# Expert combine over three engines one group apart, early beta, stores by group, unrolled limit search

## The chip, the cores and the metric

The kernel runs on one core of a Trainium2 chip. The time is that of the device for one execution, in microseconds; less is better. The engines are PE (TensorE), DVE (VectorE), ACT (ScalarE), POOL (GpSimd) and SP (SyncE, which here only issues DMAs).

## The reference

A chain of eight residual layers works on `x`, 16 sequences of 256 tokens with 128 features, in float32. Each layer is `x = x + f(layernorm(x))`: gated linear attention with a gated FFN, a linear layer with quantised operands, causal attention, a mixture of experts, rotary attention, a ternary MLP, a selective scan, and a second mixture of experts. The two mixtures matter here.

```python
# first mixture (L1_ffn): 4096 tokens, 8 experts, top 2, capacity by order of arrival
y[t] = sum_k gate[t, k] * out[expert[t, k], slot[t, k]]          # x = x + y

# second mixture (L3_ffn): capacity 768 for each expert, filled by descending gate value
pv, pp = lax.top_k(prio, capacity)                               # prio: gate value, -1 elsewhere
h     = gelu(xin @ w1 + b1);  out_e = (h @ w2 + b2) * w
out   = zeros.at[tok].add(out_e)
out   = (out - mean(out)) / sqrt(var(out) + 1e-5) * ln_g + ln_b  # x = x + out
```

## The kernel before

The program is a list of layers. Each is a `Block` in which every engine has its own written-out stream, with semaphores between the streams; a block ends in a barrier of all engines (line L57 in the profile). `sig.close()` then runs another block in which GpSimd clears the layer's semaphores one after the other. `x` stays in SBUF as 32 tiles of 128 tokens by 128 features.

`router` (for the first and, with `by_weight`, the last mixture) normalises the tiles on ScalarE, computes the logits and ranks them on VectorE. For the last mixture it then searches each expert's limit, the 768th largest gate, bit by bit: `STEPS` = 15 steps of two bits. In a step VectorE makes three candidates (`cand`), counts per candidate the values that reach it (`seen`, `counts`), PE adds the counts over partitions, and VectorE keeps the bits whose count is large enough (`keep`, `gain`, `prefix`). Both engines run the steps in a hardware loop (`Fori`), with waits whose value grows by a register. Every step depends on the one before.

`experts` runs 16 units (two halves of eight experts) of transposes, `hidden` and `result` on PE, with activations on ScalarE, `turned` (`xT`) and `result` (`y`, which adds b2) on VectorE, and scatters to `results` in DRAM by GpSimd. Its order on PE and VectorE is `turned(u+1)`, then `result(u-1)`.

After the last scatter comes the combine, in `NGROUP` = 8 groups of `GT` = 4 tiles. SP loads for each group the two expert rows of every token (`got`, three buffers) and waits from the fourth group on until `used` frees a buffer. VectorE does all else: the first product by the gate (in the first mixture with `x` added), the second product and sum, `bn_stats` and `bn_aggr` for the layernorm that follows (first mixture) or for the layernorm of the result (last mixture). In the last mixture it goes on: variance plus epsilon (`ve`), a wait for GpSimd's power -0.5 (`rs`), normalisation, times `ln_g`, plus `ln_b`, plus `x`. There is one `acc`, and a group is finished before the next begins. When all is done, a block of its own (`store`) writes `x` to the output in one DMA of 2 MB.

Of the kernel before, what the change touches and what calls it, by code (L numbers as in the profile page):

```python
# [13 lines left out]
ALU = mybir.AluOpType  # L14
# [4 lines left out]
P = 128  # L19
# [3 lines left out]
LN_EPS = 1e-5  # L23
# [1427 lines left out]
def router(nc, g, name, w, bias, by_weight, cap, queue):  # L1451
# [48 lines left out]
    with nc.Block() as block:  # L1500
        @block.vector
        def _(dve):
# [52 lines left out]
            if by_weight:  # L1555
# [11 lines left out]
                with dve.Fori(0, STEPS) as b:  # L1567
# [121 lines left out]
        def _(pe):  # L1689
# [19 lines left out]
            if by_weight:  # L1709
# [21 lines left out]
def experts(nc, g, name, w1, b1, w2, b2, last, cap, queue, results):  # L1731
# [13 lines left out]
    acc = sb("acc", [P, GT, P])  # L1745
    st, mv = sb("st", [P, GT, 6]), sb("mv", [P, GT, 2])
    rs, ve = sb("rs", [P, GT]), sb("ve", [P, GT])
# [4 lines left out]
    back, used = sig("back", 3), sig("used")  # L1752
    sum_ready, x_ready, st_ready, mv_ready, ve_ready, rs_ready, ln_ready = (
        sig("sum"), sig("x"), sig("st"), sig("mv"), sig("ve"), sig("rs"), sig("ln"))
    H, Y, T = g.pb[0:4], g.pb[4:6], g.pb[6:8]

    with nc.Block() as block:
        @block.sync
        def _(sp):
# [9 lines left out]
            for i in range(NGROUP):  # L1769
                if i >= 3:  # L1770
                    sp.wait_ge(used, i - 2)
                for k in range(2):
# [3 lines left out]
                        .then_inc(back[i % 3], 16)  # L1776

        @block.gpsimd
        def _(pool):
# [8 lines left out]
            if not last:  # L1788
                return
            with pool.Fori(0, NGROUP) as i:  # L1790
# [12 lines left out]

# [40 lines left out]
        def _(dve):  # L1844
# [12 lines left out]

            turned(0)
# [5 lines left out]
            flat = acc[:, :, :].rearrange("p t d -> p (t d)")  # L1864
            for i in range(NGROUP):
                cols = slice(i * GT * P, (i + 1) * GT * P)
                dve.wait_ge(back[i % 3], 32 * (i // 3 + 1))
                for t in range(GT):
                    gate = g.gate[:, 0, i * GT + t:i * GT + t + 1]
                    if last:  # L1870
                        ins = dve.tensor_scalar(acc[:, t, :], got[i % 3][0][:, t, :], gate, None, ALU.mult)
                    else:
                        ins = dve.scalar_tensor_tensor(out=acc[:, t, :], in0=got[i % 3][0][:, t, :], scalar=gate,
                                                       in1=g.x[:, i * GT * P + t * P:i * GT * P + (t + 1) * P],
                                                       op0=ALU.mult, op1=ALU.add)
                ins.then_inc(sum_ready, 1)
                dve.wait_ge(sum_ready, 2 * i + 1)
                for t in range(GT):
                    gate = g.gate[:, 1, i * GT + t:i * GT + t + 1]
                    out = acc[:, t, :] if last else g.x[:, i * GT * P + t * P:i * GT * P + (t + 1) * P]  # L1880
                    ins = dve.scalar_tensor_tensor(out=out, in0=got[i % 3][1][:, t, :], scalar=gate,
                                                   in1=acc[:, t, :], op0=ALU.mult, op1=ALU.add)
                ins.then_inc(sum_ready, 1)
                dve.wait_ge(sum_ready, 2 * i + 2)
                dve.memset(g.scrap[:, 0:1], 0.0).then_inc(used, 1)
                for t in range(GT):
                    out = acc[:, t, :] if last else g.x[:, i * GT * P + t * P:i * GT * P + (t + 1) * P]
                    ins = dve.bn_stats(st[:, t, :], out)
                ins.then_inc(st_ready, 1)
                dve.wait_ge(st_ready, i + 1)  # L1890
                for t in range(GT):
                    out = mv[:, t, :] if last else g.mv[:, 2 * (i * GT + t):2 * (i * GT + t) + 2]
                    ins = dve.bn_aggr(out, st[:, t, :])
                ins.then_inc(mv_ready, 1)
                dve.wait_ge(mv_ready, i + 1)
                if last:
                    dve.tensor_scalar(ve[:, :], mv[:, :, 1], LN_EPS, None, ALU.add).then_inc(ve_ready, 1)
                    dve.wait_ge(rs_ready, i + 1)
                    for t in range(GT):
                        ins = dve.tensor_scalar(acc[:, t, :], acc[:, t, :], mv[:, t, 0:1], rs[:, t:t + 1],  # L1900
                                                ALU.subtract, ALU.mult)
                    ins.then_inc(ln_ready, 1)
                    dve.wait_ge(ln_ready, i * 4 + 1)
                    dve.tensor_tensor(acc[:, :, :], acc[:, :, :],  # L1904
                                      g.l3_ln_g[:, :].unsqueeze(1).broadcast_to([P, GT, P]), ALU.mult)\
                        .then_inc(ln_ready, 1)
# [1328 lines left out]
class Globals:  # L3235
    pass


def store(nc, g, out):

    sig = Signals(nc, "store")
    stored = sig("stored")
# [179 lines left out]
```

## Time and profile before

| | |
|---|---|
| runs of the kernel | 2951.98 us median of 3 (2951.33 to 2956.23) |
| profiled execution | 2951.07 us, span 2949.2 us |
| busy: PE, DVE, ACT, POOL | 75%, 62%, 43%, 40% of the span |
| limit search | 2611.60 to 2658.96 us of the span |
| first combine, VectorE | 1402.37 to 1431.72 us |
| last combine, VectorE | 2872.89 to 2937.10 us |
| from there to the end of the span | 12.1 us |

The busy shares are means over twelve layers with different limits. The positions are microseconds from the start of the span, which is the profiled execution without what lies before and behind it on the device. A timeline merges neighbouring instructions of one line into one row with their number; the bracket gives the engine's idle time ahead of it and what ended it. "SPq" is a DMA issued by SP.

### The profile page before, as it was taken

The page shows a single profiled execution, that of the slowest core. Times are in us where ns is not written, and L with a number is a line of the kernel's source. Part 1 is how long each engine was busy: PE and PEld are TensorE (multiplying, and loading weights), DVE is VectorE, ACT ScalarE, POOL GpSimd, SP SyncE. Part 2 cuts the span into 40 slices and gives each one's busy share as a digit, 9 for nine tenths or more (in the row PEclk, how much of TensorE's full clock was granted, in tenths as well). Part 3 has the DMA queues.
Part 4 walks back from the last instruction along what each step waited for, and adds up shares of the span by engine and source line. Part 5 has one row for each costly group of instructions (what it writes and reads, how often), then busy time and mean ns, then how long its engine had stood idle before and what let it go on. Part 6 is the DMA issues. An engine that isn't in the chain of part 4 may idle for free. (4 is left out here: it accounts for less than half of the span.)

```text
span 2949.2 us, 46603 instructions
## 1 busy us (share of the span) xinstructions
PE 2197.5 (75%) x15036; PEld 1518.3 (51%) x15036; DVE 1830.9 (62%) x4981; ACT 1253.6 (43%) x2698; POOL 1185.2 (40%) x1211
## 2 busy tenths in 40 slices
PE   2799999999988885078289896959999999730480
PEld 0566666666667674056155554846666666430360
DVE  3678787878767854011656664748988888752016
ACT  1454545454523264022045553736666666320230
POOL 2433333333311002735112121557777777515441
PEclk9899999999999586589588887979999999855695
DMA  7300000000010000122323222000000000001122
GB/s 215 115 1 0 0 0 0 0 0 0 0 62 4 0 1 3 52 60 62 96 65 80 70 74 77 0 1 1 0 0 0 0 0 0 0 1 35 53 77 65
DMA packets 105859, 93.80 MB, mean 32 GB/s; under 512 B 12268, under 2 KB 92294, under 8 KB 105606
## 3 DMA queue, kind: packets, MB, share of 16 engines
q1 hardware_dynamic: 98086, 76.85, 9.4%
q0 software_dynamic: 7680, 15.81, 1.6%
q8 instruction: 47, 0.77, 0.1%
q14 instruction: 46, 0.38, 0.0%
HBM read 62.15 MB, written 46.26 MB: 37 GB/s over the span
## 5 line engine op out<-in xcount | busy, mean ns | idle before, releaser
L2993 POOL TENSOR_SCALAR mb_w<-mb_duT,mb_bT 128x256 f32<-128x256 f32 x512 | 466.8, 932 | 121.6 <-PE bank L3003 65.0
L2928 DVE TENSOR_TENSOR_SCAN mb_hs<-mb_dA,bank 128x512 f32<-128x512 f32 x256 | 300.9, 1205 | 37.8 <-issue 24.8
L38 POOL TENSOR_TENSOR scrap<-ones 128x1 f32<-128x1 f32 x64 | 12.4, 194 | 749.0 <-DVE gla_ss L420 487.0
L3022 PE MATMUL bank<-mb_hc,ident 128*128 128x512 f32 x512 | 262.2, 636 | 13.2 <-DVE mb_hc L2938 12.5
L2150 DVE TENSOR_REDUCE ra_mx<-bank 128x2 f32<-128x512 f32 x256 | 166.9, 688 | 101.9 <-PE bank L2027 100.1
L2984 ACT ACTIVATE mb_dA<-mb_delta,mb_A 128x255 f32<-128x255 f32 x512 | 216.6, 495 | 9.2 <-DVE mb_hs L2928 9.0
L2236 ACT ACTIVATE ra_pT<-bank 128x512 f32<-128x512 f32 x256 | 139.4, 595 | 131.8 <-PE bank L2047 130.7
L1801 ACT ACTIVATE e_hid<-bank,e_b 128x512 f32<-128x512 f32 (+1 forms) x128 | 81.2, 634 | 234.9 <-PE bank L1820 231.9
L3003 PE MATMUL bank<-ident,mb_w 128*128 128x128 f32 x1024 | 151.4, 282 | 34.3 <-DVE mb_hs L2928 26.2
L1812 PE MATMUL bank<-ident,e_x 128*128 128x128 f32 x112 | 18.8, 292 | 205.4 <-DMA e_x<-queue 205.4
L1784 POOL DMA_INDIRECT results<-e_y,e_x x112 | 107.2, 957 | 144.3 <-DVE e_y L1855 119.3
L2938 DVE TENSOR_TENSOR mb_hc<-mb_hs,bank 128x1024 f32<-128x1024 f32 x128 | 153.0, 1195 | 0.0
L3003 PEld LDWEIGHTS bank<-ident,mb_w 128*128 128x128 f32 x1024 | 120.7, 146 | 50.0 <-issue 34.3
L546 DVE COPY_PREDICATED gla_sT<-c_seen,bank 128x384 f32<-128x384 int32 x256 | 134.7, 579 | 12.1 <-issue 12.1
L3022 PEld LDWEIGHTS bank<-mb_hc,ident 128*128 128x128 f32 x512 | 92.9, 202 | 94.9 <-issue 67.9
L1849 DVE COPY e_xT<-bank 128x512 f32<-128x512 f32 (+1 forms) x32 | 19.7, 616 | 188.2 <-PE bank L1812 188.1
L532 DVE TENSOR_TENSOR gla_qm<-bank,gla_ex 128x256 f32<-128x256 f32 x128 | 54.0, 422 | 123.3 <-ACT gla_en L514 123.3
L1855 DVE TENSOR_TENSOR e_y<-bank,e_b 128x512 f32<-128x512 f32 (+1 forms) x32 | 20.0, 625 | 166.4 <-PE bank L1830 166.4
L2027 PE MATMUL bank<-ra_k,ra_q 48*128 48x256 bf16 x512 | 97.7, 304 | 33.8 <-DMA ra_q<-rope_rows 28.1
L1812 PEld LDWEIGHTS bank<-ident,e_x 128*128 128x128 f32 x112 | 14.4, 152 | 207.7 <-DMA e_x<-queue 206.8
L2046 PE MATMUL bank<-ra_q,ra_k 48*128 48x256 bf16 x512 | 111.4, 298 | 10.7 <-ACT ra_neg L2229 9.4
L387 ACT ACTIVATE gla_az<-gla_az 128x512 f32<-128x512 f32 x64 | 40.3, 630 | 178.6 <-DVE gla_az L415 178.6
(521 smaller groups left out, 6112.7 us busy)
## 6 DMA issues: line engine op xcount, KB each, us to landing
results<-const_empty SPq DMA_DIRECT2D x2, 4096.0 KB
e_got<-results SPq DMA_DIRECT2D x32, 256.0 KB, 3.2
rope_rows<-ra_part SPq DMA_DIRECT2D x48, 128.0 KB, 1.9
ra_k<-rope_rows SPq DMA_DIRECT2D x32, 192.0 KB, 3.3
ra_q<-rope_rows SPq DMA_DIRECT2D x32, 192.0 KB, 4.2
queue<-const_spare_rows SPq DMA_DIRECT2D x1, 4128.0 KB
e_x<-queue SPq DMA_DIRECT2D x8, 516.0 KB, 4.0
e_w<-in_L_ffn_w SPq DMA_DIRECT2D x2, 2048.0 KB, 7.8
```

Of the source, the lines that this page charges most:

```text
L546: dve.copy_predicated(sT[b][:, hd, :], g.seen[:, :], SC[hd][:, 0:3 * P]).then_inc(sc_ready, 1)
L1784: pool.indirect_dma_start(out=results[:, :], in_=y[u % YR][:, t, :], in_offset=None, out_offset=bass.IndirectOffsetOnAxis(ap=x[e % XR][:, ...
L2027: ins = pe.matmul(MX[a][:, t * 256:(t + 1) * 256], qz[k][rows, p, t * P:(t + 1) * P], kk[k][rows, p, :], start=True, stop=True)
L2046: pe.matmul(out, kk[k][rows, p, t * P:(t + 1) * P], qz[k][rows, p, :], start=True, stop=False)
L2150: dve.tensor_reduce(mx[:, :, a, p], halves(MX[a]), AXX, ALU.max).then_inc(mx_ready, 1)
L2236: act.activation(pT[p % 4][a][:, :, :], halves(SB[a]), ACT.Exp, scale=SC).then_inc(p_ready, 1)
L2928: dve.tensor_tensor_scan(hs[n // 2 % 2][:, n % 2, :, :].rearrange("p c t -> p (c t)"), dA[n % RD][:, :, :].rearrange("p c t -> p (c t)"), ...
L2938: dve.tensor_tensor(hc[grp % 2][:, :, :, :], hs[grp % 2][:, :, :, :], RC[grp % 2][:, :].rearrange("p (n t) -> p n t", n=2).unsqueeze(2) .b ...
L2984: ins = act.activation(dA[n % RD][:, c, 1:SEQ], delta[k][:, c, 1:SEQ], ACT.Exp, scale=A[:, c, n:n + 1])
L2993: ins = pool.tensor_scalar(w[n % RH][:, h, :], duT[k][:, h, :], bT[k][:, h, n:n + 1], None, ALU.mult)
L3003: ins = pe.transpose(DB[n % 2][:, c * 256 + h * P:c * 256 + (h + 1) * P], w[n % RH][:, h, c * P:(c + 1) * P], g.ident[:, :])
L3022: ins = pe.matmul(YB[:, :], g.ident[:, :], hc[grp % 2][:, j, :, :].rearrange("p c t -> p (c t)"), start=(n == 0), stop=(n == NS - 1))
```

## The change

The limit search is written out in Python loops on VectorE and PE; its instructions are the same.

In the combine, the first product goes to ScalarE (`first`, into `part`). In the first mixture GpSimd adds `x` to it (`joined`). VectorE adds the second product (`summed`) and takes the moments one group later. In the last mixture ScalarE normalises (`normalised`, as `rs * acc + nmr`, with `nmr` = -mean times rs made by VectorE in `shifts`), GpSimd takes the power (`power`) and multiplies by `ln_g` (`scaled`), and VectorE adds the result to `x` (`residual`) three groups behind. `ln_b` is added to `x` during the expert loop, one group in each of eight units (`biased`). `part`, `acc`, `st`, `mv`, `rs`, `ve` and `nmr` have three buffers. SP stores each group when its residual is done, its waits standing between those for loads; the `store` block is gone, so the layer's closing block is the last of the program. `experts` makes 30 semaphores to be cleared where it made 26.

```diff
-                with dve.Fori(0, STEPS) as b:
+                for b in range(STEPS):
...
-                with pe.Fori(0, STEPS) as b:
+                for b in range(STEPS):
...
             for i in range(NGROUP):
                 if i >= 3:
-                    sp.wait_ge(used, i - 2)
+                    sp.wait_ge(sum_ready, i - 2)
...
+                if last and i >= 4:
+                    store(sp, i - 4)
+            if last:
+                for i in range(NGROUP - 4, NGROUP):
+                    store(sp, i)
+                sp.wait_ge(stored, 16 * NGROUP)
...
+            def joined(i):
+                pool.wait_ge(part_ready, i + 1)
+                pool.tensor_tensor(flat(part[i % 3]), flat(part[i % 3]), g.x[:, cols_of(i)], ALU.add)\
+                    .then_inc(joint_ready, 1)
+
+            def power(i):
+                if i >= 3:
+                    pool.wait_ge(n_ready, i - 2)
                 pool.wait_ge(ve_ready, i + 1)
-                pool.tensor_tensor(rs[:, :], ve[:, :], g.neg_half[:, 0:GT], ALU.pow).then_inc(rs_ready, 1)
+                pool.tensor_tensor(rs[i % 3][:, :], ve[i % 3][:, :], g.neg_half[:, 0:GT], ALU.pow).then_inc(rs_ready, 1)
+
+            def scaled(i):
+                pool.wait_ge(n_ready, i + 1)
+                pool.tensor_tensor(acc[i % 3][:, :, :], acc[i % 3][:, :, :],
+                                   g.l3_ln_g[:, :].unsqueeze(1).broadcast_to([P, GT, P]), ALU.mult)\
+                    .then_inc(scaled_ready, 1)
+
+            for i in range(NGROUP + 1):
+                if not last:
+                    if i < NGROUP:
+                        joined(i)
+                    continue
+                if i < NGROUP:
+                    power(i)
+                if i:
+                    scaled(i - 1)
...
+            def first(i):
+                act.wait_ge(back[i % 3], 32 * (i // 3 + 1))
+                if i >= 3:
+                    act.wait_ge(sum_ready, i - 2)
+                for t in range(GT):
+                    ins = act.activation(part[i % 3][:, t, :], got[i % 3][0][:, t, :], ACT.Copy,
+                                         scale=g.gate[:, 0, i * GT + t:i * GT + t + 1])
+                ins.then_inc(part_ready, 1)
+
+            def normalised(i):
+                act.wait_ge(nmr_ready, i + 1)
+                for t in range(GT):
+                    ins = act.activation(acc[i % 3][:, t, :], acc[i % 3][:, t, :], ACT.Identity,
+                                         bias=nmr[i % 3][:, t:t + 1], scale=rs[i % 3][:, t:t + 1])
+                ins.then_inc(n_ready, 1)
+
+            for i in range(NGROUP + 2):
+                if i < NGROUP:
+                    first(i)
+                if last and i >= 2:
+                    normalised(i - 2)
...
+            def biased(i):
+                dve.tensor_tensor(g.x[:, cols_of(i)].rearrange("p (t d) -> p t d", d=P),
+                                  g.x[:, cols_of(i)].rearrange("p (t d) -> p t d", d=P),
+                                  g.l3_ln_b[:, :].unsqueeze(1).broadcast_to([P, GT, P]), ALU.add).then_inc(xb_ready, 1)
+
...
             for u in range(N + 1):
                 if u + 1 < N:
                     turned(u + 1)
                 if u:
                     result(u - 1)
+                if last and 1 <= u <= NGROUP:
+                    biased(u - 1)
...
+            def residual(i):
+                dve.wait_ge(scaled_ready, i + 1)
+                dve.wait_ge(xb_ready, NGROUP)
+                dve.tensor_tensor(g.x[:, cols_of(i)], flat(acc[i % 3]), g.x[:, cols_of(i)], ALU.add).then_inc(x_ready, 1)
+
+            for i in range(NGROUP + 3):
+                if last and i >= 3:
+                    residual(i - 3)
+                if i < NGROUP:
+                    summed(i)
+                if last and 2 <= i < NGROUP + 2:
+                    shifts(i - 2)
+                if 1 <= i < NGROUP + 1:
+                    moments(i - 1)
+                    gathered(i - 1)
                     if last:
+                        variance(i - 1)
```

## Rows read from the trace of the kernel before

**Rows 1.** Timeline of the limit search: start us, us, engine, line, operation.

```profile
2655.97 0.16 DVE L1571 TENSOR_TENSOR r_cand<-r_prefix,r_unit 128x3 int32<-128x3 int32 x1 [0.39 <-DVE r_prefix L1588]
...
2658.96 0.15 DVE L1591 COPY r_s<-zeros 128x1 f32<-128x1 f32 x1 [0.21 <-DVE r_prefix L1588]
```

**Rows 2.** Waits during the search: who, for whom, us, times, longest.

```profile
DVE r_cand L1571 <- DVE r_prefix L1588: 5.4, 14, 0.4
```

**Rows 3.** Timeline of the first expert layer's combine.

```profile
1402.37 1.14 DVE L1873 SCALAR_TENSOR_TENSOR e_acc<-e_got,gate,x 128x128 f32<-128x128 f32 x4 [11.83 <-DMA e_got<-results]
...
1406.05 1.14 DVE L1873 SCALAR_TENSOR_TENSOR e_acc<-e_got,gate,x 128x128 f32<-128x128 f32 x4
...
1431.34 0.38 DVE L1893 BATCH_NORM_AGGREGATE mv<-e_st 128x2 f32<-128x6 f32 x4
```

**Rows 4.** Timeline of the last expert layer's combine, its first group.

```profile
2872.89 0.87 DVE L1871 TENSOR_SCALAR e_acc<-e_got,gate 128x128 f32<-128x128 f32 x4 [10.20 <-DMA e_got<-results]
2873.80 1.14 DVE L1881 SCALAR_TENSOR_TENSOR e_acc<-e_got,gate,e_acc 128x128 f32<-128x128 f32 x4
...
2875.88 0.38 DVE L1893 BATCH_NORM_AGGREGATE e_mv<-e_st 128x2 f32<-128x6 f32 x4
2876.29 0.17 DVE L1897 TENSOR_SCALAR e_ve<-e_mv 128x4 f32<-128x4 f32 x1
2876.55 1.04 POOL L1792 TENSOR_TENSOR e_rs<-e_ve,neg_half 128x4 f32<-128x4 f32 x1 [8.99 <-DVE e_ve L1897]
2877.63 1.12 DVE L1900 TENSOR_SCALAR e_acc<-e_acc,e_mv,e_rs 128x128 f32<-128x128 f32 x4 [1.17 <-POOL e_rs L1792]
...
2880.23 0.69 DVE L1912 TENSOR_TENSOR x<-e_acc,x 128x512 f32<-128x512 f32 x1
2880.96 0.88 DVE L1871 TENSOR_SCALAR e_acc<-e_got,gate 128x128 f32<-128x128 f32 x4
```

**Rows 5.** Timeline of the tail.

```profile
2936.41 0.69 DVE L1912 TENSOR_TENSOR x<-e_acc,x 128x512 f32<-128x512 f32 x1
2940.12 0.38 SPq L3246 DMA_DIRECT2D out<-x  x1
```

**Rows 6.** The page's DMA issues: times, KB each, median us to landing.

```profile
e_got<-results SPq DMA_DIRECT2D x32, 256.0 KB, 3.2
rope_rows<-ra_part SPq DMA_DIRECT2D x48, 128.0 KB, 1.9
...
out<-x SPq DMA_DIRECT2D x1, 2048.0 KB, 8.7
```

**Rows 7.** Busy time in a stretch of the last expert loop.

```profile
2783.00:2860.00 77.00, 77.00 (x488) 62.70 (x487) 13.37 (x26) 32.08 (x56) 39.60 (x42) 1.00 0.21 62
```

**Rows 8.** Groups by line and shape: busy us, mean ns, idle before.

```profile
L1672 ACT ACTIVATE rows_or_y<-x,r_nmr,rs 128x128 f32<-128x128 f32 x64 | 27.6, 484 | 41.8 <-DVE r_nmr L1509 41.8
...
L813 ACT ACTIVATE ffn_hn<-rows_or_y,ffn_rr 128x128 f32 x24 | 8.4, 406 | 0.0
...
L641 POOL TENSOR_TENSOR e_w<-e_w,gla_az 128x2048 f32<-128x2048 f32 x16 | 72.6, 4538 | 0.0
...
L2519 POOL TENSOR_TENSOR tm_a<-tm_a 128x512 f32<-128x512 f32 x16 | 20.3, 1269 | 28.7 <-ACT tm_a L2515 28.7
...
L2955 DVE TENSOR_TENSOR mb_uc<-mb_uc,mb_gr 128x512 f32<-128x512 f32 x16 | 15.2, 950 | 0.6
...
L2808 DVE TENSOR_TENSOR mb_z<-mb_delta,mb_uc 128x512 f32<-128x512 f32 x16 | 11.1, 692 | 0.5
```

**Rows 9.** The barrier's line L57 in the tail: each queue's drain.

```profile
L57 DVEq DRAIN  x1: 10/10/10, 2938.1 to 2938.1; - x1
...
L57 POOLq DRAIN  x1: 47/47/47, 2939.8 to 2939.8; - x1
```

**Rows 10.** Timeline of ScalarE alone while the last router turns rows.

```profile
2583.62 0.37 ACT L1682 ACTIVATE r_xT<-bank 128x256 f32<-128x256 f32 x1
2583.89 0.88 ACT L1672 ACTIVATE rows_or_y<-x,r_nmr,rs 128x128 f32<-128x128 f32 x2
```

More of the change, by code:

```diff
@@ L1744, in experts @@
     got = [[sb(f"got{b}{k}", [P, GT, P]) for k in range(2)] for b in range(3)]
-    acc = sb("acc", [P, GT, P])
-    st, mv = sb("st", [P, GT, 6]), sb("mv", [P, GT, 2])
-    rs, ve = sb("rs", [P, GT]), sb("ve", [P, GT])
+    B3 = range(3)
+    part, acc = [sb(f"part{b}", [P, GT, P]) for b in B3], [sb(f"acc{b}", [P, GT, P]) for b in B3]
+    st, mv = [sb(f"st{b}", [P, GT, 6]) for b in B3], [sb(f"mv{b}", [P, GT, 2]) for b in B3]
+    rs, ve, nmr = [[sb(f"{n}{b}", [P, GT]) for b in B3] for n in ("rs", "ve", "nmr")]
     func = ACT.Gelu if last else ACT.Relu
@@ L1751, in experts, with cols_of, column, flat @@
     h_psum, h_ready = sig("hp", HC), sig("h", HC)
-    back, used = sig("back", 3), sig("used")
-    sum_ready, x_ready, st_ready, mv_ready, ve_ready, rs_ready, ln_ready = (
-        sig("sum"), sig("x"), sig("st"), sig("mv"), sig("ve"), sig("rs"), sig("ln"))
+    back = sig("back", 3)
+    names = ["part", "joint", "sum", "st", "mv", "ve", "rs", "nmr", "n", "scaled", "x", "xb"]
+    (part_ready, joint_ready, sum_ready, st_ready, mv_ready, ve_ready, rs_ready, nmr_ready, n_ready, scaled_ready,
+     x_ready, xb_ready) = [sig(n) for n in names]
+    stored = nc.alloc_semaphore(f"{name}_stored")
+    out = g.out.rearrange("b (h p) d -> p (b h) d", p=P)
     H, Y, T = g.pb[0:4], g.pb[4:6], g.pb[6:8]
     with nc.Block() as block:
+        def cols_of(i):
+            return slice(i * GT * P, (i + 1) * GT * P)
+        def column(i, j):
+            return slice((i * GT + j) * P, (i * GT + j + 1) * P)
+        def flat(ap):
+            return ap[:, :, :].rearrange("p t d -> p (t d)")
+        def store(sp, i):
+            sp.wait_ge(x_ready, i + 1)
+            sp.dma_start(out[:, i * GT:(i + 1) * GT, :],
+                         g.x[:, cols_of(i)].rearrange("p (t d) -> p t d", d=P)).then_inc(stored, 16)
         @block.sync
@@ L1876, in _ @@
[L1876 to L1906, printed above, removed]
-                    dve.wait_ge(ln_ready, i * 4 + 2)
-                    dve.tensor_tensor(acc[:, :, :], acc[:, :, :],
-                                      g.l3_ln_b[:, :].unsqueeze(1).broadcast_to([P, GT, P]), ALU.add)\
-                        .then_inc(ln_ready, 1)
-                    dve.wait_ge(ln_ready, i * 4 + 3)
-                    dve.tensor_tensor(g.x[:, cols], flat, g.x[:, cols], ALU.add).then_inc(ln_ready, 1)
-                    dve.wait_ge(ln_ready, i * 4 + 4)
@@ new lines, in summed, with moments @@
+                    to = acc[i % 3][:, t, :] if last else g.x[:, column(i, t)]
+                    ins = dve.scalar_tensor_tensor(out=to, in0=got[i % 3][1][:, t, :],
+                                                   scalar=g.gate[:, 1, i * GT + t:i * GT + t + 1],
+                                                   in1=part[i % 3][:, t, :], op0=ALU.mult, op1=ALU.add)
+                ins.then_inc(sum_ready, 1)
+            def moments(i):
+                dve.wait_ge(sum_ready, i + 1)
+                if i >= 3:
+                    dve.wait_ge(mv_ready, i - 2)
+                for t in range(GT):
+                    ins = dve.bn_stats(st[i % 3][:, t, :], acc[i % 3][:, t, :] if last else g.x[:, column(i, t)])
+                ins.then_inc(st_ready, 1)
@@ new lines, in gathered, with variance @@
+            def gathered(i):
+                dve.wait_ge(st_ready, i + 1)
+                if last and i >= 3:
+                    dve.wait_ge(nmr_ready, i - 2)
+                for t in range(GT):
+                    at = 2 * (i * GT + t)
+                    ins = dve.bn_aggr(mv[i % 3][:, t, :] if last else g.mv[:, at:at + 2], st[i % 3][:, t, :])
+                ins.then_inc(mv_ready, 1)
+            def variance(i):
+                dve.wait_ge(mv_ready, i + 1)
+                if i >= 3:
+                    dve.wait_ge(rs_ready, i - 2)
+                dve.tensor_scalar(ve[i % 3][:, :], mv[i % 3][:, :, 1], LN_EPS, None, ALU.add).then_inc(ve_ready, 1)
@@ L3376, in program @@
             layer(nc, g)
-        store(nc, g, out)
 def laid_out(inputs):
```

33 lines of the change are left out of this document (11 added, 22 removed).

## The prediction

> **What bounds the kernel now.** I read the page first for the span and the busy shares, then the chain of waits for its tail, then the timeline of the three places that the diff touches, the rows of each operation that moves to another engine, and last the DMA rows for loads and stores. The profiled execution took 2951.07 us with a span of 2949.2; the runs shown have a median of 2951.98, 0.9 above it. I sum against 2951.07 and add 0.9 at the end. No engine bounds the whole program: each layer is closed by a barrier, so each touched place counts by its own critical path, and a microsecond saved there comes off the end.
>
> The places are three. The limit search (2611.6 to 2658.96) runs 15 steps in one chain from VectorE to PE and back; in each the loop's turn shows as idle time in front of `cand` [rows 1, 2]. The combine of the first expert layer (1402.37 to 1431.72) is VectorE alone: every group starts as the one before ends, 3.67 us later [rows 3]. The combine of the last expert layer (2872.89 to 2937.10) is VectorE alone with one trip to GpSimd a group: 8.07 us for the first, 64.2 for the eight [rows 4, 5]. Behind it stand a close of 3.02 us and one 2 MB store, which lands after 8.7 us [rows 5, 6].
>
> **The search.** Unrolling takes away the loop's turn on VectorE and PE and adds no work. `cand` waits 0.39 us behind `prefix` [rows 1, 2] (14 times, 5.4 us), where dependent steps in straight-line code start some 0.04 us after the one before (2873.80 behind 2872.89 + 0.87 [rows 4]). So 14 x 0.35 = 4.9; the loop's exit (0.21 idle ahead of L1591 [rows 1]) and the entry give about 0.15 each: 5.2. PE's turn lies under VectorE's counting. Bounds: 4.2, if 0.07 of each turn stays, to 5.6. The straight-line code needs some 10 VectorE instructions in 2.8 us; in the expert loop, straight-line too, PE is fed 488 matmuls and 487 weight loads in 77.00 us and is busy for all 77.00 [rows 7]. I charge nothing for instruction supply.
>
> **The first combine.** The gate-0 product goes to ScalarE (4 Copies with a scale), the sum with x to GpSimd, and VectorE keeps the second product, bn_stats and bn_aggr. ScalarE: L813 is this instruction, 0.406 each [rows 8]; neighbours overlap by 0.1, as L1672's pairs do (0.88 for two of 0.484 [rows 8, 10]): 4 x 0.406 - 3 x 0.1 = 1.3 a group. GpSimd: 128x512 adds of this kind cost between 4.54/4 = 1.13 and 1.27 [rows 8]: 1.16, with 0.05 for a handover. VectorE: 1.12 for the four products, 0.95 for bn_stats, 0.42 for the aggregates (2874.94 to 2875.88 to 2876.29 [rows 4]) = 2.5 a group. The eight products that leave take 1.17 a group with them. The buffer ring: the load of group i+3 waits for the products of group i, both halves land 0.4 + 3.2 us later [rows 6], then 1.3 + 1.2 + 1.2: 7.3 for three groups, 2.43 each, so it just keeps up with 2.5. ScalarE's `part` buffers free at the same signal. From the first landing: 1.3 + 1.2 until VectorE starts, 8 x 2.5, and two short waits of 0.4 while the pipe fills: 23.3 instead of 29.35, so -6.0. The close has 30 semaphores to clear in place of 26; 26 take 1.7 us between VectorE's drain and GpSimd's [rows 9], so +0.26.
>
> One cost does not show in this stage: GpSimd and VectorE now work at once. The nearest rows: `mb_z` L2808, a 128x512 product from two SBUF tiles while GpSimd is idle, takes 691 ns; L2955, the same shape beside GpSimd's products, has a mean of 950 [rows 8]. So a meeting costs up to about 0.3. By my schedule about half of the joins start near the end of VectorE's products; 4 x 0.3, less what the waits absorb: +1.0. The ends are 0 and the whole join, 1.16 a group, which eats the whole gain. First combine: -6.0 + 0.26 + 1.0 = -4.7, bounds -6 to 0.
>
> The Trainium skill (page "SBUF — State Buffer", section "Who interferes with whom") speaks against this part: a VectorE instruction with two SBUF inputs and a GpSimd instruction that reads SBUF cannot run together, and the later one waits for the whole of the first. The rows show a milder stretch, 0.26 on average, so the trace agrees on the pair and not on the size. By the rule each meeting would cost up to the whole 1.16: about 3 us more in the order that I expect, and rival 1's time in the most unlucky one.
>
> **The last combine.** Per group VectorE drops the first product (0.91), the normalisation (1.15), the g product (0.73), the b sum (0.73) and the wait for `rs` (1.17) [rows 4]. ScalarE gets the first product (1.3) and the normalisation, L1672's instruction: 4 x 0.484 - 3 x 0.1 = 1.65 [rows 8, 10]. GpSimd gets g (1.16) beside `pow` (1.01 to 1.04). ScalarE now alternates Copy and Identity. It does so in the router too (L1682, then L1672, with no table load between them [rows 10]); I charge none.
>
> What sets the new period is GpSimd's order: `power(i)` stands before `scaled(i-1)`. `power` waits for `variance`, the last thing VectorE does in a turn, and VectorE's next turn begins with `residual`, which waits for `scaled`. So the turn is a ring, not an overlap: residual 0.69 + products 1.12 + shifts 0.15 + bn_stats 0.95 + bn_aggr 0.42 + variance 0.20, 0.1 for double waits, then 0.08 + 1.01 for `pow`, 0.04 + 1.16 for g: 5.92, less 0.07 where two neighbours are independent: 5.85. VectorE alone would need 3.6. ScalarE (first, then the normalisation) is done 0.8 before GpSimd comes to it. VectorE stands still while GpSimd multiplies, so nothing meets there.
>
> Fill: 1.35 (first product) + 1.12, wait 0.15, second group 1.12 + 1.57, third turn 1.12 + 0.15 + 1.57, `pow` 1.09, g 1.21 = 10.5. Then five periods to the start of residual 5: 29.25. Drain: residual 0.7, shifts 0.15, last moments 1.57, `pow` 1.1, g 1.2, residual 0.7, shifts 0.2, normalise 1.7, g 1.2, residual 0.75 = 9.3. Sum 49.1 instead of 64.2: -15.1. Bounds -13 (g at 1.27, 0.1 more a turn for waits) to -17.
>
> The sums with beta move into the expert loop: 8 x 0.69 on VectorE, behind its `y` and ahead of the next `xT`, which PE needs a unit later. PE is busy for 77.00 of 77.00 us there and VectorE for 13.37 [rows 7], so they cost nothing; with no cover they would be 5.5. `residual` waits for the last of them, long done.
>
> The stores: SP now waits for a residual before it issues the loads behind it. Load 5 is held until residual 0, where `sum_ready` alone would let it go about 5 us earlier; it lands 3.6 after that and ScalarE adds 1.3, which is some 7 us before its turn. No stall.
>
> **The tail.** Now 12.1 us from the last residual (2937.10) to the end: 3.02 close, store, 0.4 [rows 5, 6]. After: only the last 256 KB remain, between 1.9 for 128 KB and 8.7 for 2048 KB on a line 2.35 [rows 6], 0.15 to issue, then the close itself, which now lies behind the store: the drains are already in, so 1.7 + 0.26 for the clears [rows 9], 0.2 of barrier and 0.5 of waking = 2.7. Sum 5.3: -6.8, bounds -5 to -7.5.
>
> **Sum.** -5.2 - 4.7 - 15.1 - 6.8 = -31.8. 2951.07 - 31.8 = 2919.3, and with 0.9 for the median 2920.2: I say 2920. The bounds together reach 2916 to 2930.
>
> **The rivals.**
> 1. The join meets VectorE every time and the first combine gains nothing (1.16 a group comes back). For: it reads two SBUF tiles as L2955's neighbour does. Against: 0.26 in the rows, and VectorE's 1.37 of bn_stats and bn_aggr, long enough to hold it. 2920 + 5: 2925.
> 2. The last combine is bound by VectorE alone: 3.6 a turn, (5.85 - 3.6) x 6 = 13 less: 2907. For: the groups are spread one apart. Against: the order on GpSimd, written above.
> 3. Something is late in the unrolled parts: instruction supply in the search, or the loads queued behind stores on SP. Either would give back 5 to 8: 2925 to 2928. Against: PE's straight-line stretch [rows 7], and 7 us of slack.
> 4. Slower: GpSimd's product with a broadcast g is dear. Its price depends on the operation: `pow` takes 1.01 for 4 columns [rows 4]. It is in the ring, so each 1 us more costs about 7. It reaches the time before at 1.16 + 31.8/7 = 5.7 us. Against: L641 and L2519 at 1.13 to 1.27 for 512 columns [rows 8].
> 5. The change does nothing: possible only if two of the parts fail together.
>
> **How the numbers follow.** The forecast 0.72, rival 1 0.11, rival 2 0.04, rival 3 0.09, rival 4 0.02, rival 5 0.02. The range takes in the forecast's own bounds and rivals 1 and 3, and some way towards rival 2: 2912 to 2930. A measurement of this kernel tells about 0.2% (6 us) from no change. Faster 0.96, same 0.02, slower 0.02.
>
> **What would show it.** `cand` behind `prefix` with 0.04 idle; the search 42 us long. First combine 23 to 25 us, VectorE's idle time there short and before `x<-e_got`. In the last one VectorE waits for GpSimd's `acc` once a turn, about 2.2 us, residuals 5.8 to 5.9 apart; GpSimd waits for `ve`, then works `pow` and g back to back. Last residual to the end 5.3. The prediction is wrong if residuals come 3.6 apart or over 6.5, if GpSimd's g is not near 1.16, if table loads stand between ScalarE's Copy and Identity, or if the join stretches VectorE's products by more than 0.3.

## The result and the profile after

The changed kernel takes 2920.14 us (median of 4, 2915.42 to 2922.2); the kernel before, run with it, 2951.65. The ratio is 0.9893, with a 95% interval of 0.987 to 0.9915. The profiled execution took 2919.82 us with a span of 2918.0, 31.2 below the span of before.

I read it stage by stage, since the total also holds stages that the change does not touch.

| stage | before | after | difference | forecast |
|---|---|---|---|---|
| limit search (first `cand` to L1591) | 47.4 | 42.2 | -5.1 | -5.2 |
| first combine (first landing to last bn_aggr) | 29.35 | 26.0 | -3.35 | -5.0 |
| its close (to GpSimd's drain) | 2.3 | 4.3 | +2.0 | +0.26 |
| last combine | 64.2 | 49.6 | -14.6 | -15.1 |
| last residual to the end | 12.1 | 5.9 | -6.2 | -6.8 |
| all the rest | | | -3.9 | 0 |

The touched stages gave 27.3 us. The last row is in layers that no edit touches: the rotary attention went from 391.4 to 389.0 us and the selective scan from 642.2 to 638.9 from one barrier to the next, while the others moved by about 1 or less.

**The search.** The waits of VectorE in it after the change, who for whom, us, times, longest:

```profile
DVE r_keep L1581 <- PE bank L1717: 9.0, 15, 0.6
...
DVE r_limit L1593 <- PE bank L1720: 0.6, 1, 0.6
```

There is no row of `cand` behind `prefix` any more [rows 2]. The timeline shows what stands in its place, and the end of the search [rows 1]:

```profile
2646.17 0.16 DVE L1571 TENSOR_TENSOR r_cand<-r_prefix,r_unit 128x3 int32<-128x3 int32 x1
...
2648.80 0.16 DVE L1588 TENSOR_TENSOR r_prefix<-r_prefix,r_gain 128x1 int32<-128x1 int32 x1
2648.99 0.15 DVE L1591 COPY r_s<-zeros 128x1 f32<-128x1 f32 x1
```

The dependent step starts 0.03 us after the one before it. VectorE waits for PE as it did before: 9.0 us in 15 steps.

**The first combine.** Timeline of VectorE, ScalarE and GpSimd after the change, where [rows 3] showed VectorE alone:

```profile
1405.07 1.28 ACT L1855 ACTIVATE e_part<-e_got,gate 128x128 f32<-128x128 f32 x4 [19.00 <-DMA e_got<-results]
...
1407.72 1.28 ACT L1855 ACTIVATE e_part<-e_got,gate 128x128 f32<-128x128 f32 x4 [1.38 <-DMA e_got<-results]
1407.80 1.14 DVE L1947 SCALAR_TENSOR_TENSOR x<-e_got,gate,e_part 128x128 f32<-128x128 f32 x4 [14.59 <-POOL e_part L1815]
...
1410.44 2.19 DVE L1947 SCALAR_TENSOR_TENSOR x<-e_got,gate,e_part 128x128 f32<-128x128 f32 x4 [1.50 <-POOL e_part L1815]
1410.69 1.26 POOL L1815 TENSOR_TENSOR e_part<-e_part,x 128x512 f32<-128x512 f32 x1 [0.35 <-ACT e_part L1855]
1412.55 0.86 DVE L1957 BATCH_NORM_STATS2 e_st<-x 128x6 f32<-128x128 f32 x4
...
1413.74 2.11 DVE L1947 SCALAR_TENSOR_TENSOR x<-e_got,gate,e_part 128x128 f32<-128x128 f32 x4
1414.11 1.33 POOL L1815 TENSOR_TENSOR e_part<-e_part,x 128x512 f32<-128x512 f32 x1 [2.16 <-ACT e_part L1855]
...
1416.97 1.11 DVE L1947 SCALAR_TENSOR_TENSOR x<-e_got,gate,e_part 128x128 f32<-128x128 f32 x4
...
1419.99 1.14 DVE L1947 SCALAR_TENSOR_TENSOR x<-e_got,gate,e_part 128x128 f32<-128x128 f32 x4 [0.72 <-POOL e_part L1815]
...
1423.42 0.86 DVE L1957 BATCH_NORM_STATS2 e_st<-x 128x6 f32<-128x128 f32 x4
1423.44 1.26 POOL L1815 TENSOR_TENSOR e_part<-e_part,x 128x512 f32<-128x512 f32 x1 [1.19 <-ACT e_part L1855]
...
1430.69 0.38 DVE L1966 BATCH_NORM_AGGREGATE mv<-e_st 128x2 f32<-128x6 f32 x4
```

The four products of a group (L1947) take 1.11 to 1.14 us, but 2.19 and 2.11 where GpSimd's sum (L1815, 1.26) starts beside them. bn_stats, which reads one tile, keeps its 0.86 with the sum beside it (1423.42 and 1423.44). VectorE waits 1.50 ahead of the second group, whose load ScalarE itself had to wait for. The turns without a meeting, from 1416.97 on, are 2.4 to 3.0 long. The row of the four single products of the second group (ns: shortest, median, longest) shows where its 2.19 comes from:

```profile
L1947 DVE SCALAR_TENSOR_TENSOR x<-e_got,gate,e_part x4: 340/346/1390, 1410.4 to 1412.3; 128x128 f32<-128x128 f32 x4
```

Three of the products are untouched. One, which came just as GpSimd's sum began, took 1.39.

**The last combine.** One turn of the timeline, where [rows 4] showed a group:

```profile
2885.45 0.69 DVE L1985 TENSOR_TENSOR x<-e_acc,x 128x512 f32<-128x512 f32 x1 [2.42 <-POOL e_acc L1826]
...
2886.28 1.14 DVE L1947 SCALAR_TENSOR_TENSOR e_acc<-e_got,gate,e_part 128x128 f32<-128x128 f32 x4
...
2887.33 0.15 DVE L1979 SCALAR_TENSOR_TENSOR e_nmr<-e_mv,e_rs 128x4 f32<-128x4 f32 x1
2887.41 0.86 DVE L1957 BATCH_NORM_STATS2 e_st<-e_acc 128x6 f32<-128x128 f32 x4
2887.53 1.65 ACT L1862 ACTIVATE e_acc<-e_acc,e_nmr,e_rs 128x128 f32<-128x128 f32 x4 [3.04 <-DVE e_nmr L1979]
2888.30 0.38 DVE L1966 BATCH_NORM_AGGREGATE e_mv<-e_st 128x2 f32<-128x6 f32 x4
2888.72 0.17 DVE L1973 TENSOR_SCALAR e_ve<-e_mv 128x4 f32<-128x4 f32 x1
2889.03 1.01 POOL L1822 TENSOR_TENSOR e_rs<-e_ve,neg_half 128x4 f32<-128x4 f32 x1 [3.61 <-DVE e_ve L1973]
2889.08 1.26 ACT L1855 ACTIVATE e_part<-e_got,gate 128x128 f32<-128x128 f32 x4
2890.01 1.26 POOL L1826 TENSOR_TENSOR e_acc<-e_acc,l_ln_g 128x512 f32<-128x512 f32 x1
2891.30 0.69 DVE L1985 TENSOR_TENSOR x<-e_acc,x 128x512 f32<-128x512 f32 x1 [2.41 <-POOL e_acc L1826]
```

Residuals come 5.85 us apart. VectorE stands idle for 2.41 and is released by GpSimd's g (L1826), which runs right behind its `pow` (L1822). ScalarE is finished with the normalisation at 2889.18, 0.83 before GpSimd comes to it.

**The expert loop and the tail.** The row of the loop in the table of busy time by stretch, after the change, beside [rows 7]:

```profile
2772.00:2849.00 77.00, 77.00 (x485) 62.43 (x484) 17.79 (x34) 32.49 (x56) 41.72 (x42) 1.00 0.21 63
```

PE is busy for 77.00 of 77.00 us as before, with VectorE at 17.79 in place of 13.37. From the barrier ahead of the layer to the first landing of its combine it takes 106.0 us, and took 106.4. The last instructions in the timeline after the change, beside [rows 5]:

```profile
2910.11 1.26 POOL L1826 TENSOR_TENSOR e_acc<-e_acc,l_ln_g 128x512 f32<-128x512 f32 x1 [2.56 <-ACT e_acc L1862]
2911.41 0.69 DVE L1985 TENSOR_TENSOR x<-e_acc,x 128x512 f32<-128x512 f32 x1 [3.05 <-POOL e_acc L1826]
```

After the last residual (2912.10) the drains follow at 2915.6 and GpSimd's, behind the clears, at 2917.7, as the rows of line 57 show (ns of one, then the times of the first and the last):

```profile
L57 DVEq DRAIN  x1: 19/19/19, 2915.7 to 2915.7; - x1
...
L57 POOLq DRAIN  x1: 47/47/47, 2917.7 to 2917.7; - x1
```

### The profile page after: what moved, and what is told of

It reads as the page before. It is cut to its first block and busy times, and to the rows that moved or that the text cites. A ratio compares the mean times of both kernels' runs of the same rounds, so it can differ in the third digit from the quotient of the medians.

```text
span 2918.0 us, 46463 instructions
## 1 busy us (share of the span) xinstructions
PE 2191.5 (75%) x15036; PEld 1514.7 (52%) x15036; DVE 1800.3 (62%) x4869; ACT 1285.8 (44%) x2794; POOL 1206.7 (41%) x1227
## 5 line engine op out<-in xcount | busy, mean ns | idle before, releaser
L3107 PE MATMUL bank<-mb_hc,ident 128*128 128x512 f32 x512 | 255.9, 624 | 16.0 <-DVE mb_hc L3023 15.9
L546 DVE COPY_PREDICATED gla_sT<-c_seen,bank 128x384 f32<-128x384 int32 x256 | 134.6, 578 | 12.2 <-issue 12.1
```

The source lines that it names most:

```text
L546: dve.copy_predicated(sT[b][:, hd, :], g.seen[:, :], SC[hd][:, 0:3 * P]).then_inc(sc_ready, 1)
L3107: ins = pe.matmul(YB[:, :], g.ident[:, :], hc[grp % 2][:, j, :, :].rearrange("p c t -> p (c t)"), start=(n == 0), stop=(n == NS - 1))
```

## The experiments

All are told by stage, from one profile each, since totals of single runs differ by more than most edits here. "Combine" is from the first landing (ScalarE's or VectorE's first product) to VectorE's last instruction.

How far one profile can be read differs from stage to stage. The search (42.2) and the last stretch (5.9) repeat to 0.1. The last combine lies between 49.5 and 50.0 in all profiles that leave its order alone. The first combine does not repeat well: in the seven profiles with three load buffers and nothing altered in that stage it took 25.0, 25.4, 25.7, 25.9, 26.0, 26.5 and 27.4, and two to four of its eight groups met GpSimd.

### The search alone

```diff
 # kernel before
-                with dve.Fori(0, STEPS) as b:
+                for b in range(STEPS):
-                with pe.Fori(0, STEPS) as b:
+                for b in range(STEPS):
```

> The kernel before with the limit search alone written out. My theory: the loop's turn is all that goes, 0.35 us in each of 14 steps and some 0.3 at the two ends: the steps come 2.82 us apart (3.17 before), the search is 5.2 shorter, and the rest of the program keeps its stage times. Rival: what the changed kernel also saved outside the touched stages (some 3 us in the rotary attention and the selective scan) comes with this edit; then those stages are shorter here too.

Measured: from the first `cand` (2610.8) to L1591 (2653.0) 42.2 us, the last router's layer 187.0 (192.2 before, 186.6 in the changed kernel). The rotary attention took 397.7 us here and the scan 637.2, against 391.4 and 642.2. So the edit is worth 5.1 to 5.3, all of it in its stage, and the untouched stages move by 5 or 6 us, one up and one down, in a kernel that differs from the one before by two lines.

### g ahead of the power on GpSimd

```diff
 # changed kernel
+                if i:
+                    scaled(i - 1)
                 if i < NGROUP:
                     power(i)
-                if i:
-                    scaled(i - 1)
```

> The changed kernel with one swap in GpSimd's stream: scaled(i-1) stands ahead of power(i). My theory (the ring through GpSimd's order sets the turn): the ring is then residual 0.69, products 1.06, shifts 0.1, normalise 1.65, g 1.26 and handovers of 0.2, so residuals come 4.95 us apart in place of 5.85, and the combine ends 5 us earlier. Rival (VectorE and GpSimd are held by something else, as a load or ScalarE's order): the turn stays at 5.85.

Measured: residuals 5.09 apart (4.95 expected), combine 45.0 us, 4.6 less than in the changed kernel. The timeline of the edited kernel:

```profile
2883.90 0.69 DVE L1985 TENSOR_TENSOR x<-e_acc,x 128x512 f32<-128x512 f32 x1 [1.66 <-POOL e_acc L1826]
...
2885.97 1.65 ACT L1862 ACTIVATE e_acc<-e_acc,e_nmr,e_rs 128x128 f32<-128x128 f32 x4 [2.28 <-DVE e_nmr L1979]
...
2887.70 1.26 POOL L1826 TENSOR_TENSOR e_acc<-e_acc,l_ln_g 128x512 f32<-128x512 f32 x1 [2.86 <-ACT e_acc L1862]
2888.92 1.01 POOL L1822 TENSOR_TENSOR e_rs<-e_ve,neg_half 128x4 f32<-128x4 f32 x1
2888.99 0.69 DVE L1985 TENSOR_TENSOR x<-e_acc,x 128x512 f32<-128x512 f32 x1 [1.65 <-POOL e_acc L1826]
```

g now runs when the normalisation is done (2885.97 + 1.65), and VectorE waits 1.65 in place of 2.41. That shows the cause of the turn of 5.85: the order of two instructions on GpSimd.

### The residual at the end of the turn

```diff
 # changed kernel; acc has four buffers, acc[i % 4]
-                if last and i >= 3:
+                if last and i >= 4:
-                    dve.wait_ge(x_ready, i - 2)
+                    dve.wait_ge(x_ready, i - 3)
...
             for i in range(NGROUP + 3):
-                if last and i >= 3:
-                    residual(i - 3)
                 if i < NGROUP:
                     summed(i)
...
                         variance(i - 1)
+                if last and i >= 3:
+                    residual(i - 3)
...
-                if last and i >= 4:
-                    store(sp, i - 4)
             if last:
-                for i in range(NGROUP - 4, NGROUP):
+                for i in range(NGROUP):
                     store(sp, i)
```

> The changed kernel with four acc buffers, the residual at the end of VectorE's turn in place of its start, and the stores behind all loads. The ring is gone. If VectorE and GpSimd do not disturb each other, the turn is VectorE's own 3.5 us. If an instruction of one waits for the whole of the other's when both read two SBUF tiles, the turn is at least VectorE's products and sums (1.9) and GpSimd's pow and g (2.3) one after the other: 4.2. Either way the combine ends 10 to 14 us earlier than in the changed kernel. Rival: the turn stays above 5, and the order was not the bound.

Three things change here at once: the place of the residual, the number of `acc` buffers and the place of the stores. (The kernel with one store, below, shows that the place of the stores does not move this combine.) Measured: combine 44.7, 4.9 less, with a turn of 5.10: half of what was expected. The old ring is gone and another stands there:

```profile
2889.95 0.86 DVE L1955 BATCH_NORM_STATS2 e_st<-e_acc 128x6 f32<-128x128 f32 x4
2890.06 1.65 ACT L1860 ACTIVATE e_acc<-e_acc,e_nmr,e_rs 128x128 f32<-128x128 f32 x4 [2.29 <-DVE e_nmr L1977]
...
2891.61 1.26 ACT L1853 ACTIVATE e_part<-e_got,gate 128x128 f32<-128x128 f32 x4
2892.86 1.26 POOL L1824 TENSOR_TENSOR e_acc<-e_acc,l_ln_g 128x512 f32<-128x512 f32 x1
2892.96 2.10 DVE L1945 SCALAR_TENSOR_TENSOR e_acc<-e_got,gate,e_part 128x128 f32<-128x128 f32 x4 [0.94 <-ACT e_part L1853]
```

VectorE's products wait 0.94 for ScalarE's first product (L1853), which stands behind the normalisation (L1860), which waits for the turn's shifts. And the products take 2.10 in place of 1.14, with GpSimd's g beside them.

### The first product further ahead

```diff
 # kernel of the experiment before
+            first(0)
             for i in range(NGROUP + 2):
-                if i < NGROUP:
-                    first(i)
+                if i + 1 < NGROUP:
+                    first(i + 1)
```

> The kernel of lag4, with ScalarE's first product one group further ahead: first(i+1) stands before normalised(i-2). In lag4 the turn was 5.10 us, and VectorE waited 0.93 for the first product, which stood behind the normalisation. My theory: lag4 was bound by that ring (products 2.10 with GpSimd in the way, shifts, normalise 1.65, first product 1.26), so the wait goes and the turn falls to 4.2 to 4.5, VectorE's own work plus about 1 us in which its products stand behind GpSimd's instruction. Rival: VectorE and GpSimd exclude each other so often that the turn stays near 5.

Measured: turn 4.35, combine 41.1. VectorE no longer waits; what it loses is inside its products, which take 2.14 with GpSimd's g beside them:

```profile
2887.84 2.14 DVE L1946 SCALAR_TENSOR_TENSOR e_acc<-e_got,gate,e_part 128x128 f32<-128x128 f32 x4
2888.55 1.29 POOL L1824 TENSOR_TENSOR e_acc<-e_acc,l_ln_g 128x512 f32<-128x512 f32 x1
```

In the single run the total was 2918.5, above the 2914.8 of the kernel without this edit, although the last layer is 3.7 us shorter: the rotary attention took 396.5 us here and 390.6 there.

### What holds VectorE's products

```diff
 # changed kernel, first combine only: the sum with x is left out
-                pool.tensor_tensor(flat(part[i % 3]), flat(part[i % 3]), g.x[:, cols_of(i)], ALU.add)\
+                pool.memset(flat(acc[i % 3]), 0.0)\
                     .then_inc(joint_ready, 1)
```

> The changed kernel, with GpSimd's join in the first combine replaced by a memset of a spare tile of the same size: x is not added there. GpSimd then writes SBUF and reads nothing. If VectorE's two products of 2.19 and 2.11 us (1.14 elsewhere) were held by GpSimd's reads, all eight now take 1.14. If they were held by GpSimd's writes, or by the landing loads, long ones remain. The first combine gets 2 to 4 us shorter (a memset may be quicker than the join).

All eight groups' products took 1.10 to 1.14 us, and the combine 21.7, 4.3 less (2 to 4 were expected). But the memset is short (0.52) and fell beside bn_stats or ahead of the products each time, so this run shows that GpSimd's sum is the cause and not whether its reads are. Two more kept the sum and added work behind it:

```diff
 # changed kernel, first combine, behind each join: writes only
+                if i:
+                    pool.wait_ge(n_ready, 2 * i)
+                for k in range(2):
+                    pool.memset(flat(acc[k]), 0.0).then_inc(n_ready, 1)
```

> The changed kernel; in the first combine GpSimd, after each join, also writes two spare tiles (memset, 0.52 us each), just when VectorE's products of the same group begin. These instructions read nothing and are on nobody's path but GpSimd's own. My theory: only an instruction of GpSimd that reads SBUF holds up a VectorE instruction with two SBUF inputs. Then the products beside the memsets take 1.14 us, and the combine stays within 1 us of 26.0. Rival: any GpSimd work on SBUF does it; then most products take about 2 us, and the combine lasts 30 or more.

```diff
 # changed kernel, first combine, behind each join: an instruction that reads
+                if i:
+                    pool.wait_ge(n_ready, i)
+                pool.tensor_tensor(flat(acc[2]), w1[:, 0, :], w1[:, 1, :], ALU.add).then_inc(n_ready, 1)
```

> The changed kernel; in the first combine GpSimd, after each join, also adds two tiles of weights into a spare tile (128x512, 1.26 us). It reads SBUF, just when VectorE's products of the same group begin. My theory: the products of most groups now take about 2.2 us in place of 1.14, the whole of GpSimd's instruction lying between them, and the combine lasts 30 us or more (26.0 in the changed kernel). If the stretch is the mild one that I took for the prediction (0.26), the products take 1.4 and the combine 27 to 28.

The timeline of the kernel with the added writes:

```profile
1419.80 0.99 POOL L1820 MEMSET e_acc<- 128x512 f32 x2
1419.97 1.14 DVE L1951 SCALAR_TENSOR_TENSOR x<-e_got,gate,e_part 128x128 f32<-128x128 f32 x4 [0.23 <-POOL e_part L1815]
```

And that of the kernel with the added reads:

```profile
1420.42 1.26 POOL L1819 TENSOR_TENSOR e_acc<-e_w 128x512 f32<-128x512 f32 x1
1420.57 4.07 DVE L1950 SCALAR_TENSOR_TENSOR x<-e_got,gate,e_part 128x128 f32<-128x128 f32 x4 [0.94 <-POOL e_part L1815]
...
1421.92 1.29 POOL L1815 TENSOR_TENSOR e_part<-e_part,x 128x512 f32<-128x512 f32 x1 [0.24 <-ACT e_part L1858]
...
1423.18 1.31 POOL L1819 TENSOR_TENSOR e_acc<-e_w 128x512 f32<-128x512 f32 x1
...
1425.72 1.25 POOL L1819 TENSOR_TENSOR e_acc<-e_w 128x512 f32<-128x512 f32 x1
1425.75 2.17 DVE L1950 SCALAR_TENSOR_TENSOR x<-e_got,gate,e_part 128x128 f32<-128x128 f32 x4
```

Beside the memsets (0.99 for the pair) the products keep their 1.14, in five of the eight groups. The second and third take 2.19 and 2.11 as in the changed kernel; there a join still stands beside them. The combine lasts 25.8, within the spread of kernels without the memsets.

Beside sums that read, five of the eight groups are stretched: the first two together took 7.11, three more 4.07, 2.17 and 3.06, and three met nothing. Inside the 4.07 lie three of GpSimd's instructions. Single products that met one took 1.25 to 1.38 in place of about 0.34, eleven of the 32. The combine lasts 32.6, far outside the spread. So GpSimd's sum of two SBUF tiles lets the VectorE product that is already running finish and holds the next one almost to its own end; an instruction that only writes does not. For this pair the mild price of my prediction is refuted.

### Four buffers for the loads

```diff
 # changed kernel; got, part and back have NB = 4 buffers
-                if i >= 3:
-                    sp.wait_ge(sum_ready, i - 2)
+                if i >= NB:
+                    sp.wait_ge(sum_ready, i - NB + 1)
...
-                if i >= 3:
-                    act.wait_ge(sum_ready, i - 2)
+                if i >= NB:
+                    act.wait_ge(sum_ready, i - NB + 1)
```

> The changed kernel with four buffers for the loads and for part in place of three, in both combines. My theory: in the first combine the later turns (2.4 to 2.8 us) were set by the ring of loads; now they take VectorE's own 2.3, and the combine ends 1 to 2 us earlier (24 to 25 us from the first landing, 26.0 in the changed kernel). In the last combine nothing changes: residuals 5.85 apart. Rival: the landings do not set these turns; the first combine keeps 26.0.

Measured: first combine 25.1 (26.0), last one 49.75 with residuals as before. The length alone shows nothing, since kernels with three buffers took 25.0 to 27.4. The rows show more: VectorE's waits for joins after the second group are gone, and turns of 2.22 appear, VectorE's own work, where with three buffers no full turn was under 2.36. Three groups' products now meet GpSimd (2.15, 2.00 and 2.35) in place of two. So the ring of loads did lengthen the later turns, and a good part of that comes back as meetings.

### The tail

```diff
 # changed kernel, experts: no clearing block behind the last layer
     sb.close()
-    sig.close()
+    if last:
+        sig.ctx.close()
+    else:
+        sig.close()
```

> The changed kernel without the block that clears the last layer's 30 semaphores, as the old store block had none. My theory: in the changed kernel that block lies behind the last store, between the drains at 2915.6 and the end, so the time from the last residual to the end falls from 5.9 to 3.7 us. Rival: the end is set by the store's completion, and 5 us or more remain.

```diff
 # changed kernel: one store when all is done
-                if last and i >= 4:
-                    store(sp, i - 4)
             if last:
-                for i in range(NGROUP - 4, NGROUP):
-                    store(sp, i)
-                sp.wait_ge(stored, 16 * NGROUP)
+                sp.wait_ge(x_ready, NGROUP)
+                sp.dma_start(out[:, :, :], g.x[:, :].rearrange("p (t d) -> p t d", d=P)).then_inc(stored, 16)
+                sp.wait_ge(stored, 16)
```

> The changed kernel with one store of 2 MB when all residuals are done, in place of eight. My theory: the store lands 8.7 us after its issue as in the kernel before, and the clears stay behind it: 12.2 us from the last residual to the end (5.9 with stores by group), and residuals still 5.85 apart. Rival: the stores by group disturb the loads or the queue, and the combine is shorter without them.

Measured, from the last residual to the end of the span: 3.5 us without the clears, 11.5 with the single store, 5.9 in the changed kernel. So the stores by group are worth 5.6, and the clears that now lie bare cost 2.4. With one store the last combine is still 49.6: the stores by group do not disturb it. The DMA row of the store in the kernel with one store (KB each, median us from issue to landing):

```profile
out<-x SPq DMA_DIRECT2D x1, 2048.0 KB, 8.7
```

and in the changed kernel, over the same stretch:

```profile
out<-x SPq DMA_DIRECT2D x4, 256.0 KB, 2.3
```

### The changed kernel again, and all together

> The changed kernel once more, unaltered, on the chip of the next run. Its stages should repeat: search 42.2, first combine 26.0, last combine 49.6, last residual to the end 5.9, 2920 us in all. What differs between its profile and the others in the stages that no edit touches tells how far a total can be read.

Measured: 2923.78 us (median of 5, 2922.8 to 2930.7; 2920 expected), ratio to the kernel before 0.9912 (0.9899 to 0.9926). Its last combine is 49.8, the tail 5.9, the first combine 26.5. This is 27.5 us below the 2951.24 of the kernel before on that chip, which is what the touched stages give.

The last kernel joins the four edits: residual at the end of the turn with four `acc` and the stores behind the loads, first product further ahead, four load buffers, no clearing block behind the last layer. Its diff is the sum of those above.

> The changed kernel with everything that the runs so far point to: residual at the end of the turn with four acc buffers, stores behind the loads, first product a group ahead on ScalarE, four buffers for the loads, no clearing block behind the last layer. Its stages should add up: last combine 41 us in place of 49.6, first combine 25 in place of 26.0, 2.3 off the close: 12 us less than the changed kernel, about 2908, and a ratio to the kernel before of 0.985. Rival: with four load buffers the last combine meets GpSimd more often, and some of it comes back.

Measured: 2909.51 us (median of 4, 2904.84 to 2913.89), ratio 0.9862 (0.9844 to 0.9879). Last combine 40.5, first combine 25.4, last residual to the end 3.5. It is faster than both kernels; its slowest run is below the fastest of the changed kernel on the same chip.

## Why the prediction was right, and where it was not

The total was forecast as 2920 and measured as 2920.14. That is closer than the working deserves. The touched stages gave 27.3 us of the 31.8 that I summed, and untouched stages happened to give the rest. In the profiles of the edited kernels the rotary attention takes 388.5 to 397.7 us and the scan 635.4 to 639.6, with no edit in either. Run again, the changed kernel was 27.5 below the one before.

- **The search** was right in mechanism and size: 0.35 a step, -5.1 in the stage and about 0.15 at its entry, repeated by the edit alone. Nothing was late in the written-out code.
- **The last combine** was right: GpSimd's order sets the turn, forecast 5.85, measured 5.85, and the swap moved it to 5.09. The terms inside were off by little and cancelled: g cost 1.26 where I took 1.16, bn_stats 0.86 where I took 0.95. The fill was longer: 11.3 to the first residual where I had 10.5, since the second group's load was waited for. So rival 4, a dear g, is out. Rival 2, VectorE alone at 3.6, did not occur, and the experiments show that it could not be had by lifting that order alone: behind it stand ScalarE's order (5.10) and then GpSimd's reads (4.35).
- **The first combine** is where the prediction failed: -3.35 instead of -5.0, and by terms that were further off than that. I had 2.5 to VectorE's start, 8 x 2.5 of work, 0.8 of waits and 1.0 of meetings: 24.3. Measured were about 2.7, 8 x 2.22, 3.5 and 2.0: 26.0. The work was costed too high by 2.2 (products, bn_stats and aggregates follow each other in 1.02, 0.90 and 0.30, where I had 1.12, 0.95 and 0.42), and this hid more than half of the rest.
  - *The waits* were the largest miss. "Two short waits of 0.4 while the pipe fills": the first was 1.5, since the second group's load landed 2.65 after the first's and ScalarE stood waiting for it. And the ring of loads, which "just keeps up", held later turns at up to 3.0.
  - *The price of a meeting* was the other. I took "a meeting costs up to about 0.3" from L2955 and set it against the rule that the later instruction waits for the whole of the first. Two meetings cost 1.05 and 0.97, and the added reads show almost the whole length each time. Rows of the kernel before, which the prediction does not use, show both prices (the third row is ns: shortest, median, longest):

```profile
1857.19 0.72 POOL L2523 TENSOR_TENSOR tm_a2s<-tm_a 128x256 f32<-128x256 f32 x1
1857.26 0.68 DVE L2537 TENSOR_TENSOR tm_m<-tm_nm 128x2 f32<-128x2 f32 x1
L2955 DVE TENSOR_TENSOR mb_uc<-mb_uc,mb_gr x16: 691/992/1032, 2009.7 to 2564.6; 128x512 f32<-128x512 f32 x16
```

  L2537, a product of two SBUF inputs, takes 0.16 alone and 0.61 to 0.82 in the 15 of its 16 turns in which GpSimd adds two tiles: it is held almost to the end of the sum. L2955 also meets GpSimd 15 times out of 16, and takes 0.88 to 1.03 then against 0.69 for the last, which is alone. So 0.3 is a true price, but of a meeting with L2993, GpSimd's product of one 128x256 tile by a column (0.92). The join is a sum of two tiles as L2537's neighbour is. I read the price from the row with VectorE's shape, where GpSimd's instruction made the difference. What in L2993 makes it milder, its inputs, its operation or its size, no run tells. The Trainium skill (page "SBUF — State Buffer", section "Who interferes with whom") was right for the join in both halves, that the pair excludes each other and that a GpSimd instruction that only writes does not; for L2955 its "whole instruction" is more than the trace shows.
  - *Rival 1*, a meeting in every group, did not occur: the slots fell so that two of eight met, and two to four in the other profiles. That they were few was luck. By the prediction's own sign, a join that stretches the products by more than 0.3, this part was wrong, though the total was not.
- **The close of the first expert layer**, costed at +0.26, came to +2.0. From VectorE's drain to GpSimd's it took 2.3 in place of 1.7. The rest lies ahead of the drains: VectorE's drain follows its last instruction by 0.5 us before the change and by 2.0 after; in other runs by 0.3 (four load buffers), 0.9 (the changed kernel again) and 2.9 (added writes). Run again, the same kernel's close came to +0.9, so more than half of the +2.0 is not a fixed price of the change. No run tells what is late there, and that stays open.
- **The tail**: -6.2 against -6.8. The last store took 3.5 from the residual to the drains, where I had 3.0 with the waking, and the clears are as costed within 0.2. Rival 3, loads late behind stores, did not occur: with no store between them the combine keeps its length.
- **The beta sums** cost nothing: PE is busy for 77.00 of 77.00 us with them.

## What to carry to other kernels

When work is spread over engines one group apart, write out for each engine's queue which item stands in front of which: here the turn was set three times in a row by an order inside one queue, and lifting one showed the next. A two-operand operation that moves from VectorE to GpSimd can still hold VectorE: here it held products of two SBUF tiles for about 1 us each and left bn_stats alone, so put GpSimd's reads beside instructions of that kind. Take the price of a meeting from a row in which the other engine's instruction is of the kind that you add. Where an edit touches 5% of the program, add up its stages: the untouched ones moved by several us from build to build.

## What the runs showed of the hardware

- A GpSimd sum of 1.26 us that reads SBUF lengthened VectorE's four products from 1.14 to 2.1 or 2.2 us, and three such instructions in a row to 4.07. Memsets of 0.99 us beside the same products left them at 1.14. Even VectorE's smallest product of two SBUF tiles (`nmr`, 128x4, 0.16) took 1.22 behind g. The other way round, `pow` went from 1.01 to 1.32 beside a residual. GpSimd's product of one 128x256 tile by a column (0.92) cost VectorE's 128x512 product only 0.2 to 0.3.
- One SBUF input does not always protect VectorE: bn_stats kept its 0.86 beside a sum, but a copy of 128x4 (L2575 of the kernel before) took up to 1.26 beside GpSimd's 128x512 sum, and 0.17 alone.
- Copy and Identity alternated on ScalarE in the last combine with no table load between them, and ScalarE's normalisation of four tiles took 1.65 us as worked out.
- The same stages in kernels that differ elsewhere varied by up to 9 us in 390 (rotary attention). What sets this is not shown here.
